# Scaling weight pieces on GpSimd in place of ScalarE, in a delta-rule attention and mixture-of-experts kernel

## What is computed

```python
x = x + attn(layernorm(x))          # delta rule:
#   S_t = S_{t-1} + k_t (beta_t * (v_t - k_t^T S_{t-1}))^T ;  o_t = q_t^T S_t
# then the experts, on layernorm(x):
probs = softmax(x @ router_w.T); vals, idx = top_k(probs, 2)
for eid in range(8):
    w = sum(where(idx == eid, vals, 0), axis=-1)
    h = gelu(x @ w1[eid].T)          # 256 -> 1024
    out += w[:, None] * (h @ w2[eid].T)   # 1024 -> 256
x = x + out
```

## Time and profile before

| what | value |
|---|---|
| time, median of 3 runs | 1042.83 us (1041.49 to 1043.53) |
| the profiled execution | 1041.38 us, of which the span of its instructions 1039.0 |
| TensorE (matmul) busy | 894.5 us, 86% |
| TensorE weight loads busy | 703.7 us, 68% |
| VectorE busy | 653.1 us, 63% |
| ScalarE busy | 630.4 us, 61% |
| GpSimd busy | 434.3 us, 42% |
| mean granted TensorE clock | 0.951 of full speed |

### The profile page before, as it was taken

How to read it: one execution, slowest core, us unless ns; L and a number is a source line. 1 busy time by engine, 2 the same in 40 slices (tenths; PEclk the granted TensorE clock), 3 DMA queues, 4 the chain that set the end, 5 groups by cost and what they waited for, 6 DMA issues and landing times.

```text
span 1039.0 us, 30043 instructions
## 1 busy us (share of the span) xinstructions
PE 894.5 (86%) x9932; PEld 703.7 (68%) x9933; DVE 653.1 (63%) x1844; ACT 630.4 (61%) x1663; POOL 434.3 (42%) x433
## 2 busy tenths in 40 slices
PE   0689998888988888899973199999999999999993
PEld 0468876777767777677862077777777777777771
DVE  3378896787877878788863245545545555455551
ACT  4578887788877878777751264545545455454450
POOL 2445555556566565654434112232223322333232
PEclk9999999999999999999985599999999999999997
DMA  5112322223222232211104803332333223332222
GB/s 190 53 55 75 83 60 82 80 81 93 68 91 89 79 89 69 87 63 38 48 32 155 146 17 47 58 46 42 55 46 55 43 45 56 46 52 45 46 37 25
DMA packets 53018, 69.29 MB, mean 67 GB/s; under 512 B 6769, under 2 KB 37490, under 8 KB 52914
## 3 DMA queue, kind: packets, MB, share of 16 engines
q1 hardware_dynamic: 37394, 47.82, 16.3%
q0 software_dynamic: 14432, 19.02, 11.2%
q10 hardware_dynamic: 1088, 1.07, 0.6%
HBM read 42.41 MB, written 25.47 MB: 65 GB/s over the span
## 4 chain that ended last, share of the span: by engine, by line
PE 65%; DVE 8%; POOL 8%; issue 6%; ACT 4%; DMA 3%; SPq 0%; DVEq 0%; POOLq 0%; ACTq 0%
PE ps L919 61%; POOL routed_rows L600 3%; ACT w_s L650 2%; PE ps L1290 2%; DVE w_s L1478 2%; POOL rs L527 1%; DMA out<-wvg_s,yidx 1%; PE ps L1005 1%; DMA tile_experts_dram<-tab_f 1%; POOL w_lo L576 1%; POOL Ll L584 1%; ACT k_sq L689 1%; PE ps L1167 1%; PE ps L951 1%; DVE rowA L1569 1%
## 5 line engine op out<-in xcount | busy, mean ns | idle before, releaser
L634 POOL DMA_INDIRECT out<-wvg_s,yidx x78 | 125.7, 1612 | 331.4 <-DVE wvg_s L1761 181.4
L919 PE MATMUL ps<-w_s,wqk 128*128 128x128 f16 (+1 forms) x1392 | 262.2, 296 | 2.0 <-DVE wvg_s L1761 2.0
L919 PE MATMUL ps<-x_s,w_hi 128*128 128x256 f16 x1248 | 208.3, 274 | 0.0
L650 ACT ACTIVATE w_s<-ps 128x512 f16<-128x512 f32 (+2 forms) x288 | 144.6, 523 | 46.9 <-PE ps L919 39.1
L919 PE MATMUL ps<-x_s,w_lo 128*128 128x256 f16 x624 | 170.9, 274 | 0.0
L1740 DVE SCALAR_TENSOR_TENSOR KpAT<-KQ,wqk 128x512 f16<-128x512 f32 x156 | 108.0, 692 | 98.8 <-ACT wqk L650 98.8
L919 PE MATMUL ps<-w_s,KpAT 128*128 x624 | 170.1, 273 | 0.0
L919 PEld LDWEIGHTS ps<-w_s,wqk 128*128 128x128 f16 x1392 | 113.3, 102 | 81.5 <-issue 5.7
L919 PEld LDWEIGHTS ps<-x_s,w_hi 128*128 x1248 | 122.6, 98 | 14.8 <-issue 0.4
L650 ACT ACTIVATE x_s<-ps 128x512 f16<-128x512 f32 x39 | 23.3, 597 | 176.3 <-PE ps L1290 176.3
L895 ACT ACTIVATE KQ<-ps 128x512 f32<-128x512 f32 x156 | 93.3, 598 | 38.3 <-PE ps L919 34.0
(11 more groups left out here) (179 smaller groups left out, 1829.5 us busy)
## 6 DMA issues: line engine op xcount, KB each, us to landing
wst<-w SPq DMA_DIRECT2D x56, 256.0 KB, 2.7
rowA<-routed_rows SPq DMA_DIRECT2D x39, 260.0 KB, 2.8
w_s<-eye SPq DMA_DIRECT2D x32, 256.0 KB, 2.7
x_s<-x SPq DMA_DIRECT2D x32, 128.0 KB, 2.6
out<-x_s SPq DMA_DIRECT2D x32, 128.0 KB, 1.7
KQ<-w SPq DMA_DIRECT2D x6, 256.0 KB, 4.2
out<-wvg_s,yidx POOLq DMA_INDIRECT x78, 3.9
routed_rows<-nL ACTq DMA_DIRECT2D x4, 260.0 KB, 11.2
```

The source lines that it names most:

```text
L634: pool.indirect_dma_start(out=out, out_offset=bass.IndirectOffsetOnAxis(ap=yidx[:, q, a:a + 1], axis=0), in_=yrow[:, q % 2, a, :], in_offs ...
L650: return act.activation(dst, src, ACT.Copy, scale=scale)
L919: return pe.matmul(dst, lhsT, rhs, start=start, stop=stop, **kw)
```

## The change

GpSimd multiplies the piece in `wst` by 256, in place, directly ahead of its own subtraction, and waits for that instruction (new semaphore `s_wscaled`) before it subtracts. `scale_piece` goes from ScalarE's order at both places. ScalarE's signal `s_whi` is now sent by the copy of the high part. Nothing else moves.

```diff
+        s_wscaled = sem("w_scaled")
...
                 pool.wait_ge(s_whi, j + 1)
+                pool.tensor_scalar(wst[:, :], wst[:, :], W_SCALE, None, ALU.mult).then_inc(s_wscaled, 1)
+                pool.wait_ge(s_wscaled, j + 1)
                 which, at = piece_of(j)
...
-                evac(dst, src, W_SCALE)
-
-            def scale_piece(j):
-                if not 0 <= j < EARLY:
-                    return
-                evac(wst[:, :], wst[:, :], W_SCALE).then_inc(s_whi, 1)
+                evac(dst, src, W_SCALE).then_inc(s_whi, 1)
...
                 kT_evac(i - 2)
-                scale_piece(2 * (i) + 0)
                 tanh_g(i - 2)
...
                 logits_copy(i - 5)
-                scale_piece(2 * (i) + 1)
                 x_evac(i - 2, 1)
```

## The result

The changed kernel takes 1100.43 us (median of 4, 1095.72 to 1102.53) against 1042.95, a ratio of 1.0547 (95% interval 1.0511 to 1.0583). The prediction was 1056.5, at most 1066. The direction was right, and so was the place; three sizes were wrong: the duration of the scaling, the number of falls of TensorE's clock, and the first ten iterations. Where the time went is seen best in TensorE's first transposes, one pair per iteration (L947 in this kernel, L951 before).

The account below looks back on a forecast made before the run. GpSimd's queue ahead of ln1, for which TensorE's router product waits, was taken as the bound. 10.0 (queue) + 0.9 (loads) - 0.5 (relief) + 3.3 (clock) = 13.7 us on 1042.8 gave 1056.5 us, range 1048.5 to 1066.

Parts of the forecast that it names:

- many falls of the clock, or a dear scaling: Rival: five to nine more iterations at half clock, or a scaling of 1.16 us; about 1064 us, chance 0.17.
- The bound and the path: Attention loop: GpSimd's queue through the subtraction and LayerNorm scale holds ScalarE's ln1, then TensorE's router product, in nine of 17 iterations.
- C, D and A: Attention iterations with i mod 4 = 3, 0, 1; forecast to pay for GpSimd's delay, slack none, none and 0.1 us.
- The duration of the scaling: GpSimd's new 128x512 multiply, taken as 0.70 us, bounds 0.53 to 1.16, plus a wait of 0.10.
- The queue's part: Even piece's 0.80 us in GpSimd's queue ahead of ln1: 9 x 0.80 plus 4 x 0.70, together 10.0 us.
- TensorE's clock, two more falls: Longer router-product waits drop TensorE to half clock, 1.63 us each; two more taken, 3.3 us, between 0 and 14.7.
- the 17 iterations: Attention iterations i = 11 to 27, which have both GpSimd's scatter of routed rows and the weight pieces.
- B: Attention iterations with i mod 4 = 2; slack of 1.0 us was to cover the even piece's delay, cost 0.
- The piece loads and the start-up: Odd piece's load lands 0.80 us later in i = 4 to 7, cost 0.9 us; start-up relief at i = 3, 0.5.
- ScalarE's relief: ScalarE loses 56 passes, 34.8 us busy; counted as a gain of 0.5 us, at start-up (i = 3) only.
- VectorE against GpSimd: A iterations: VectorE's L1569, held up by GpSimd's subtraction, gets through about 0.45 us sooner; counted 0.
- The odd piece's zero cost: Odd piece's subtraction ends up to 1.0 us later, covered by kscale's 2.2 us waits for VectorE; cost 0.

Follow-up runs that it names:

- e1: Changed kernel, but only the even pieces scaled by GpSimd, the odd ones by ScalarE as before; ratio 1.0546 to the kernel before.
- e9: Changed kernel with spare TensorE products ahead of the router product in C, D and A and ahead of the score products in B; ratio 1.0196.
- e10: Kernel before with spare TensorE products ahead of the router product in C and D and ahead of the score products in B; ratio 0.9917.
- e14: e4 with spare TensorE products ahead of the router product in C, D and A and ahead of the score products in B; ratio 1.0072.
- e4: Kernel before, ScalarE still scaling, with GpSimd also multiplying each piece by 1.0 over 180 columns (0.67 us) and waiting; ratio 1.0307.
- e5: Changed kernel with 36 spare TensorE products ahead of the router product in C, D and A; ratio 1.0219.
- e13: Changed kernel with ScalarE's high part of the odd piece moved behind the level 5 evacuation and the logits copy; ratio 1.0470.
- e3: Kernel before, ScalarE still scaling, with GpSimd also multiplying each piece by 1.0 over all 512 columns and waiting; ratio 1.0567.
- e2: Changed kernel, but only the odd pieces scaled by GpSimd, the even ones by ScalarE as before; ratio 1.0031 to the kernel before.
- e6: Kernel before with 22 spare TensorE products ahead of the router product in C and D only; ratio 0.9980.

## Why the direction was right and the size wrong

The sum of the prediction was 10.0 + 0.9 - 0.5 + 3.3. Its rival "many falls of the clock, or a dear scaling", about 1064 with a chance of 0.17, named what happened, but priced the two one at a time; they came together. Against the sum:

- **The bound and the path**: right. C, D and A pay, in front of ln1, and TensorE's router product waits (e1, and its counterpart).
- **The duration of the scaling, 0.70, at most 1.16**: wrong, 1.50. The failing step is "nearer the one-operand row, since it reads one operand", and the bound from the two-operand subtraction. No row of before showed this form, and a one-operand arithmetic instruction is not bounded by a two-operand one here (1.50 against 1.04 and 1.16). The nearest row of its kind, the one column of 268 ns, says nothing on the time per column, and the MEMSETs' 0.84 ns a column is a third of the 2.5 ns a column between 256 columns (0.85 us) and 512 (1.50).
- **The queue's part**: the working was right, the input wrong. With 1.60 in place of 0.80 it gives 9 x 1.6 + 4 x 1.5 + 4 x 0.6 = 22.8; e9 less e10 measured 288.9 - 267.9 = 21.0. At the assumed duration it is 9.4 (e14) for 10.0.
- **TensorE's clock, two more falls, 3.3 us**: this step failed most, and even its upper bound, 14.7, was too low. e9 and e10 take the falls out: they cost 324.3 - 288.9 = 35.4 us in the changed kernel and 275.4 - 267.9 = 7.5 before, so 27.9 us of the 48.9 in the 17 iterations. These are four single traces; the timed ratios of the same four kernels (1.0547 - 1.0196, less 1 - 0.9917) give 28 us for the whole kernel. The mechanism had been named and priced per fall (1.63); its number was guessed from the four C that had stayed at full clock with a wait of 1.43. They were no sign of room: 0.77 us more was enough in e4 for 72 us at half clock. The fifth C, i = 11, had fallen, which the prediction doesn't say: it lasted 18.36 us, with a wait of 1.46 and twice D's time at half clock (6.8 against 3.4 us). Its windows in the kernel before:

```profile
178.00:180.00 2.00, 2.00 (x26) 2.00 (x27) 0.70 (x4) 0.81 (x4) 0.94 (x1) 0.50 0.04 8
180.00:182.00 2.00, 2.00 (x12) 1.11 (x10) 0.85 (x2) 0.95 (x3) 0.21 (x1) 0.50 0.37 103
```

  So the price of 1.63 per fall was that of the short kind; i = 11 was 2.9 us longer than a C without one. In the changed kernel ten of the 13 C, D and A had some 6.8 us at half clock, and two of the four B (i = 18 and 22) had some too.
- **The piece loads and the start-up, 0.9 - 0.5**: too small. The first ten iterations lost 9.4. Some 1.9 lie ahead of i = 1 (first transposes 20.45 before, 22.37 changed; 21.3 to 21.5 in e5, e9 and e13, which are the changed kernel up to there): in the first iteration the even piece stands in front of ln1's scale as well. i = 5 to 8 lost 4.8, of which e13 gave back 2, and i = 9 and 10 gained 0.5. i = 1 to 4 lost 3.1. TensorE was at half clock for 14 us of the first ten iterations against 7 before; no run filled a wait there, so the share of the clock is open. At 0.67 us of dose it was still 3.9 us.
- **ScalarE's relief, 0.5**: e3 against the changed kernel can't tell it from nothing.
- **VectorE against GpSimd**: the row moved as was said; that this is worth nothing in A wasn't tested by itself. The row of L1569, L1565 here, went from 1.17 to 0.63 as the scaling came first with a gap behind it:

```profile
L1565 DVE TENSOR_SCALAR rowA<-r x8: 158/630/633, 148.9 to 622.8; 128x4 f32<-128x4 f32 x8
```

The odd piece's zero cost was right in the 17 iterations (e2). Of the whole, by these traces, 21.0 us is GpSimd's queue, 27.9 the falls, and 9.4 the first ten; together 58.3. With 2.7 for one fall in i = 30, and 1.7 us less in all that follows, that is the 59.3 us by which the spans differ (1098.3 and 1039.0). At 0.67 us (e4) the loss was 32 us, and the prediction would still have been less than half of it, mostly for the clock: against the 3.3 us that it took for more falls, the timed ratios give 24.5 in e4 less 8.6 in the kernel before, 16 us.

## What to carry to other kernels

Where TensorE waits in front of a step, price a longer wait twice: once for the wait, and once for the stretch at half clock behind it; a wait that hasn't brought a fall yet is no evidence of room, and in e4's trace 0.8 us more brought one in 11 of the 13 C, D and A iterations, where four of them had one before. An instruction form that the trace doesn't show needs a range beyond its neighbours on that engine. An engine that is idle for two fifths of a stretch can still be the one whose queue closes most iterations, so ask first what stands behind the new instruction in its order; here moving one subtraction out of that place gave 1.3%.

## What the runs showed of the hardware

- GpSimd's TENSOR_SCALAR with a constant over 128x512 f32 took 1.50 us alone (an addition) and in the loop (a product), 0.85 over 256 columns and 0.67 over 180; a product with a repeated column took 1.04 over 512 and 0.72 over 256; a copy of 256 columns 0.39.
- Spare products in TensorE's waits made the unchanged kernel 0.8% faster (0.9893 to 0.9942) and the changed one 3.3% (1.0547 to 1.0196), with no other change. The mean granted clock was 0.945 to 0.954 in the executions of the unchanged kernel and 0.952 to 0.962 with the products; in those of the changed kernel 0.916 to 0.924 and 0.955 to 0.959.
- Filling one wait can move the fall to another (e6), so the gain showed only with the waits in B filled too (e10).
